# Eight-head attention layer: the second half of the sums turned earlier in the next step, low parts ahead of the values, loop rounds of twelve steps

## The reference

```python
Wh = (h @ W).reshape(b, n, H, HD).transpose(0, 2, 1, 3)
e1 = jnp.einsum('bhnd,d->bhn', Wh, a1)
e2 = jnp.einsum('bhnd,d->bhn', Wh, a2)
e = e1[:, :, :, None] + e2[:, :, None, :]
e = jnp.where(mask, -jnp.inf, e)
e = jnp.where(e >= 0, e, ALPHA * e)
attn = jax.nn.softmax(e, axis=-1)
h_prime = jnp.einsum('bhij,bhjd->bhid', attn, Wh)
...
x = _layernorm(x + _L0_gnn_ref(x, adj, L0_gnn_W, L0_gnn_a), axis=-1)
```

## Time and profile before

| | us |
|---|---|
| median of 3 runs | 788.59 (786.36 to 789.25) |
| the profiled execution | 786.59 |
| its span | 781.4 |
| TensorE busy | 697.0 (89%) |
| VectorE busy | 616.6 (79%) |
| ScalarE busy | 555.6 (71%) |
| GpSimd busy | 399.0 (51%) |

### The profile page before, as it was taken

The page is one execution under the profiler, slowest core; times in us unless marked ns, Lnnn a source line. Parts: engine busy times, 40 slices in busy tenths (PEclk is TensorE's granted clock), DMA queues, the critical chain, the costliest instruction groups (busy, mean ns, idle before and its releaser), DMA issues.

```text
span 781.4 us, 26071 instructions
## 1 busy us (share of the span) xinstructions
PE 697.0 (89%) x8484; PEld 513.6 (66%) x8484; DVE 616.6 (79%) x1786; ACT 555.6 (71%) x1270; POOL 399.0 (51%) x615
## 2 busy tenths in 40 slices
PE   5898999989998689989949999969999999999992
PEld 4566666666665467767738999936666666666661
DVE  2688788887888769999987888866787877778765
ACT  3565666656665489999848999837878777787871
POOL 5577778787787424454431111105546464555541
PEclk9999999999999799999969999969999999999996
DMA  6343333433322213322222333401222222222211
GB/s 170 83 104 73 96 92 76 101 70 98 86 44 43 27 15 36 39 34 34 34 54 55 87 89 81 88 1 21 57 48 54 49 52 60 45 56 47 56 49 42
DMA packets 34906, 47.75 MB, mean 61 GB/s; under 512 B 4388, under 2 KB 18472, under 8 KB 34856
## 3 DMA queue, kind: packets, MB, share of 16 engines
q0 software_dynamic: 18576, 21.01, 16.8%
q1 hardware_dynamic: 15992, 25.97, 10.9%
q10 hardware_dynamic: 288, 0.13, 0.1%
HBM read 51.32 MB, written 8.39 MB: 76 GB/s over the span
## 4 chain that ended last, share of the span: by engine, by line
PE 54%; DVE 25%; issue 9%; ACT 8%; DVEq 3%; DMA 0%; ACTq 0%; POOL 0%; SPq 0%; POOLq 0%
PE banks L1175 7%; DVE pp L573 7%; PE banks L1490 5%; PE banks L1501 4%; PE banks L1474 4%; PE banks L1516 4%; PE banks L1464 4%; PE banks L1469 4%; DVE pp L896 3%; PE banks L1508 3%; PE banks L1183 3%; PE banks L692 3%; DVE stats L585 3%; PE banks L1458 2%; DVE oo L907 2%
## 5 line engine op out<-in xcount | busy, mean ns | idle before, releaser
L573 DVE SCALAR_TENSOR_TENSOR pp<-banks,floor,adj 128x1024 f32<-128x1024 f32 x128 | 157.5, 1249 | 6.9 <-PE banks L679 4.4
L1258 POOL TENSOR_TENSOR pp<-pp,adj 128x512 f32<-128x512 f32 x64 | 73.3, 1162 | 135.0 <-ACT pp L1299 135.0
L490 ACT COPY rows<-banks 128x640 bf16<-128x640 bf16 x64 | 44.3, 692 | 67.0 <-PE banks L669 66.9
L1299 ACT ACTIVATE pp<-banks,nobound 128x512 f32<-128x512 f32 x128 | 81.4, 695 | 3.5 <-PE banks L1490 1.8
L692 PE MATMUL banks<-pp,yv 128*17 128x128 f32 x2048 | 82.4, 280 | 1.3 <-DVE pp L573 1.3
L798 POOL TENSOR_TENSOR yres<-oo,x 128x512 f32 (+1 forms) x32 | 40.8, 1276 | 69.0 <-DVE oo L914 69.0
L679 PE MATMUL banks<-rows 32*128 32x128 bf16 x1024 | 51.2, 219 | 20.4 <-DVE pp L573 18.7
L1175 PE MATMUL banks<-w2b,xt 128*128 128x256 f32 x256 | 62.3, 387 | 0.0
L409 POOL TENSOR_TENSOR yv<-wh,yv 128x512 f32<-128x512 f32 x32 | 35.1, 1098 | 46.6 <-ACT yv L483 46.6
L1036 POOL DMA_DIRECT2D adj<-in_adj x32 | 17.0, 531 | 80.4 <-ACT sq L1074 80.4
L495 ACT COPY ot<-banks 128x512 f32<-128x512 f32 x64 | 37.3, 583 | 28.4 <-PE banks L692 28.4
(11 more groups left out here) (208 smaller groups left out, 1938.3 us busy)
## 6 DMA issues: line engine op xcount, KB each, us to landing
adj<-in_adjt POOLq DMA_DIRECT2D x96, 128.0 KB, 3.0
xt<-in_xt SPq DMA_DIRECT2D x32, 256.0 KB, 3.8
x<-in_x SPq DMA_DIRECT2D x32, 256.0 KB, 3.2
adj<-in_adj POOLq DMA_DIRECT2D x32, 256.0 KB, 3.0
out_ngd<-yres SPq DMA_DIRECT2D x32, 256.0 KB, 2.0
ident<-in_ident ACTq DMA_DIRECT2D x1, 64.0 KB, 2.3
w0t<-in_w0t SPq DMA_DIRECT2D x1, 64.0 KB, 2.1
w0e<-in_w ACTq DMA_DIRECT2D x1, 64.0 KB, 2.3
```

The costliest lines, as they stand in the source:

```text
L490: nc.scalar.copy(rows[:, slot % 2, a, :], R[:, 0:5 * N]).then_inc(s["rw"], 1)
L573: nc.vector.scalar_tensor_tensor(pp[:, g], S[g % 2][:, :].rearrange("p (h n) -> p h n", n=N), floor[:, slot:slot + 1], adj[:, slot, g:g + ...
L1258: nc.gpsimd.tensor_tensor(pp[:, slot % 2, h], pp[:, slot % 2, h], adj[:, slot], ALU.mult).then_inc(s["pm"], 1)
L1299: nc.scalar.activation(pp[:, slot % 2, h], S[h][:, :], ACT.Exp, bias=k["nobound"][:, :], scale=SCALE).then_inc(s["p"], 1)
```

## The change

On ScalarE the copy of the second turned half moves ahead of bases and factors; on TensorE its turn moves ahead of scores 3 and sums 1. On GpSimd the low parts move ahead of the values. The four engines' loop body becomes twelve steps, so there are two rounds in place of six. SyncE's own loop of loads is as it was. One blank line is added near the top, so a line of the code behind it has a number higher by one after the change (L573 becomes L574).

```diff
-def steps(eng, body, end=LOOP1, ring=RING):
+def steps(eng, body, end=LOOP1, ring=RING, laps=1):
     for t in range(LOOP0):
         body(t, t % ring, t // ring)
-    with eng.Fori(0, (end - LOOP0) // ring) as i:
-        for r in range(ring):
+    with eng.Fori(0, (end - LOOP0) // (ring * laps)) as i:
+        for r in range(ring * laps):
             s = LOOP0 + r
-            body(i * ring + s, s % ring, i + s // ring)
+            body(i * (ring * laps) + s, s % ring, i * laps + s // ring)
...
             if in2:
                 load_adj(t + 2, a2)
                 high(t + 2, a2)
+            if in2:
+                low(t + 2, a2)
             if not known(t) or t + 1 < T:
                 values(t + 1, a1)
-            if in2:
-                low(t + 2, a2)
...
-        steps(pool, step, end)
+        steps(pool, step, end, RING, 3)
...
             if in3:
                 copy_shift(t + 3, a3)
+            if not known(t) or t >= 1:
+                evac_turned(t - 1, c0, 1)
             if in1:
                 bases(t + 1, a1)
             if in3:
                 factors(t + 3, a3)
             evac_sums(t, 0)
-            if not known(t) or t >= 1:
-                evac_turned(t - 1, c0, 1)
...
             if in3:
                 top_column(t + 3, a3)
+            if not known(t) or t >= 1:
+                turn(t - 1, 1)
             scores(t, 3, slot)
             attend(t, 1, slot)
-            if not known(t) or t >= 1:
-                turn(t - 1, 1)
             if in4:
                 hidden(t + 4, 0, slot, lap + 1)
```

More of the change, by code:

```diff
@@ L547, in step @@
                 const.bounds(act)
-        steps(act, step, end)
+        steps(act, step, end, RING, 3)
         evac_sums(T - 1, 1)
@@ L622, in step @@
                 const.folded(dve)
-        steps(dve, step, end)
+        steps(dve, step, end, RING, 3)
         dve.wait_ge(s["stats"], T - 2)
@@ L759, in step @@
                 const.folds(pe)
-        steps(pe, step, end)
+        steps(pe, step, end, RING, 3)
         turn(T - 1, 1)
```

## The result

The changed kernel is slower by 0.6%: median 792.99 us (792.04 to 793.13, 5 runs) against 788.59 before (786.36 to 789.25), ratio 1.0062, 95% interval 1.0047 to 1.0077. The prediction, 783.7 with a range of 779 to 788.5, missed on the other side.

What follows compares the result with a forecast made beforehand. VectorE's reciprocal waiting for ScalarE's copy of the turned sums, with the lane maximum's copy close behind as second limit. Terms -0.7 - 4.2 - 2.0 + 2.0 = -4.9 us, against the median 788.59 giving 783.7, range 779 to 788.5.

Steps and rivals of the forecast that it cites:

- The hole: VectorE's 1.28 us idle before the reciprocal in a loop step: falls to 0.31, some 0.9 reappearing before the lane maximum.
- The last steps: Steps 28 to 31, without projection or lane maximum: the reciprocal comes earlier, saving 4.2 us, bounds 1.8 and 4.9.
- The saved jumps: Loop's jumps back between rounds, five reduced to one: 4 x 0.50 = 2.0 us saved, bounds 1.7 and 2.2.
- The low parts ahead of the values: GpSimd's reorder in each step: taken as 0, since the readers come a step later; bounds 0 and -0.03 a step.
- Rival D: Loop steps: ScalarE's copy of sums 0, pushed back 0.47 us, delays the weighted sums; 793.3 us at 0.4 late; 8%.
- The step's term: The 24 loop steps under the new order: each gains 0.03 us, -0.7 in all, bounds -3.1 to +1.9.
- 0.2 us of slack: Loop step: ScalarE's second copy, which the lane maximum needs, ends only 0.21 us before the maximum runs.
- The bound of 0.08 lost: Loop step's worst case: a TensorE delay of 0.14 us and 0.15 of latency lose 0.08 a step.
- The other bound: Loop step's best case: no TensorE delay and 0.03 us of latency gain 0.13 a step.
- The fetch's term: The one jump back of the twelve-step body: an instruction fetch stalls once, taken as 2.0 us, bounds 0.0 and 7.4.
- the price of one ordinary load: At the jump back: fetch priced from a 256 KB load's 3.9 us, half taken, 2.0, as TensorE's wait covers some.
- Rival C: At the jump back: several engines miss in turn, then a lower clock, 6.5 us in place of 2.0, giving 788.2; 22%.

Runs made afterwards that it cites:

- e2: Kernel before with only the loop bodies lengthened to rounds of twelve steps, old order kept: 790.60 us, ratio 1.0028.
- e8: Kernel before with only GpSimd's low parts moved ahead of the values: 787.21 us, ratio 0.9991.
- e1: The changed kernel's three moves with rounds of four steps kept, against the kernel before: 787.95 us against 788.11, ratio 0.9996.
- e5: Kernel before with only the loop bodies lengthened to rounds of eight steps, old order kept: 800.91 us, ratio 1.0156.
- e3: Kernel before with rounds of twelve on TensorE only, the other engines keeping four, old order: 793.87 us, ratio 1.0067.
- e4: Kernel before with rounds of twelve on VectorE, ScalarE and GpSimd, TensorE keeping four, old order: 789.23 us, ratio 1.0010.
- f1: Kernel before plus the three moves, rounds of four, and VectorE's lane maximum moved into the next step: 762.22 us, ratio 0.9676.

## Why the prediction was wrong

**Right.** The hole moves: 1.28 became 0.30 (forecast 0.31) before the reciprocal, and 0.90 (forecast 0.9) before the maximum. The last steps gave 4.8 (forecast 4.2), in part by luck: a share of it is the higher clock in step 31. The saved jumps count 2.0 (4 x 0.5); by e2's 0.59 a jump they gave 2.4. The low parts ahead of the values did nothing (e8). Rival D did not occur: the turned copy, at 101.44, was in time, and the copy of sums behind it ended 0.19 ahead of the weighted sums that need it (103.05, 103.24), where 0.1 was forecast. That the time came out near D's 793.3 is chance: its mechanism had no part in it.

**The step's term, -0.7 forecast, +3.4 measured (0.14 in place of -0.03 a step).** The sign hung on 0.2 us of slack, and two terms were mis-sized. The projection now follows sums and takes 0.69 until the next scores (102.22 to 102.91), where I carried over the 0.59 that it took behind the turn; so the second transposes came 0.18 late and not 0.10. And once the maximum itself waits, weights 0 follow it after 0.25 (105.32 to 105.57) and not after 0.16 as in the earlier trace rows: the small register instructions ahead of them no longer run beside the statistics. Against that the hand-over from ScalarE's copy to the maximum took 0.04 (105.28 to 105.32) and not 0.08. On these rows the step is 7.54 against 7.43: 0.02 more up to the column maximum, 0.18 to the second transposes, 0.09 behind the maximum, 0.17 less at the hand-over. The bound of 0.08 lost was too narrow: it held a TensorE delay of 0.14 at most and nothing behind the maximum. The other bound has a slip: no delay and 0.03 of latency put the maximum at 112.53, a gain of 0.18 and not 0.13, so 4.3 over 24 steps. e1 shows this term alone against the last steps' gain, no net change; by its loop the term is 4.2, so the split between steps and jumps is good to some 0.8 us.

**The fetch's term, 2.0 forecast, 7.7 measured** (8.2 less an ordinary jump's 0.5). This failed most. I took one load's time from an ordinary DMA row. The runs show two stalls in a row on an engine (TensorE of e5: some 2.0 and 2.36, of e3: 3.11 and 2.00; ScalarE after: 2.8 twice), on several engines (e3, e4), and then TensorE for 10 us at the lower clock. The step that failed is the price of one ordinary load, 2.0, partly hidden, with no term for a second miss or for the clock behind it. Rival C named this chain with 6.5. The 7.7 is read from one execution; in the old order most runs lose some 3 us less at the jump than e2's profiled one, if the jump is where they differ, which no row shows. The rule of the Trainium skill on this ("Runtime: NRT & Kernel Launch", "Instruction fetch mechanics": a taken branch whose target lies outside the window that the engine holds stalls on a fetch) is borne out as to the stall. A body of four steps of TensorE (1069 recorded instructions) stays, one of eight (2122) does not. The 2048 instructions that the Trainium skill gives TensorE there lie between the two; its window of two blocks of 256 instructions, by an estimate 512, would have made the four-step body miss too, and the earlier trace rows show no packet for it from 70 to 218 us.

**Left out: +2.0 behind the layer.** In the profile after, the granted clock was low for 13.7 us from the layer's end on, 0.66 in place of 0.79 in the stretch shown, and that stretch took 18.67 in place of 16.84. The trace of f1 has the same (13.7 us low, 18.74); in all other traces the stretch takes 16.6 to 17.0, in e1 too, with the same end (0.80, 16.96). So the loss goes with the clock; what sets how long it stays low I did not test.

In sum, for the profiled execution: -0.7, -4.2, -2.0 and 2.0 were forecast; 3.4 (and 0.4 in steps 26 and 27), -4.8, -2.0, 7.7 and 2.0 were measured, 6.7 against 6.6 in the spans (4.4 in the medians).

## What to carry to other kernels

When a wait goes, compute the second limit to a tenth of a microsecond before counting the gain, and move that one too: the same moves were worth nothing with the lane maximum at the end of the step, and came to 3.2% together with its move. A change whose parts differ in sign is worth taking apart: the moves in the last four steps alone gave 0.8%. A piece of TensorE work has no fixed price: it depends on its neighbour, so take the interval from a row with the same pair. Lengthen a loop's body only while it stays resident: look for instruction packets behind the first round, and price a miss at several microseconds and a clock drop.

## What the runs showed of the hardware

In the profiled executions a jump back to instructions no longer held costs 5.1 us (e4) to 8.3 (e2) a time, with single stalls of 2.0 to 3.4 on the engines that miss. In these counts the weight loads and the sequencer's instructions are included: TensorE's body of 1069 recorded instructions loops without a fetch (before), one of 2122 does not (e5); VectorE's body of 246 does (e5), one of 363 does not (e4). With eight steps TensorE alone misses. The engines of one kernel may loop over bodies of different length (e3, e4), and each misses by its own body's length.
